# Decoder layer on one core: cross-attention queries and keys projected compactly and spread into 32-row strips through DRAM, queries one step ahead, blank rows written over three steps

## The reference

```
q = x1  @ q_w + q_b      # x1, ctx: [8, 256, 256]
k = ctx @ k_w + k_b      # 16 heads of 16 features
v = ctx @ v_w + v_b
a = softmax(q k^T / sqrt(16))          # per head, 256 x 256
x2 = layernorm(x1 + (a v) @ o_w + o_b)
# then: logits = x2 @ gate_w, best 2 of 8 experts, rows of x2 sorted by expert
```

## Time and profile before

| | |
|---|---|
| median of 3 runs | 996.15 us (994.75 to 998.77) |
| span of the profiled execution | 1000.6 us, 18366 instructions |
| PE busy in it | 883.4 us (88%) |
| DVE, ACT, POOL busy | 632.2, 431.9, 343.5 us |
| the slowest and only core's granted clock, mean | 0.946 |
| DMA | 123.54 MB, mean 123 GB/s |

### The profile page before, as it was taken

One profiled execution on the slowest core, in us unless ns is written; L12 is line 12 of the kernel. 1 busy time (PEld: TensorE's weight loads), 2 busy tenths in 40 slices (PEclk: granted clock), 3 DMA queues, 4 the chain that ended last, 5 costly groups with the idle time before them and its releaser, 6 DMA issues.

```text
span 1000.6 us, 18366 instructions
## 1 busy us (share of the span) xinstructions
PE 883.4 (88%) x6859; PEld 660.2 (66%) x6859; DVE 632.2 (63%) x1488; ACT 431.9 (43%) x781; POOL 343.5 (34%) x318
## 2 busy tenths in 40 slices
PE   7799788779889898889889998979997999999995
PEld 5576566657667675668656555555785777777774
DVE  5799797667898888752656778774553343333255
ACT  5688565335545544433134444445331322222221
POOL 9322201022555455620201223223631142222584
PEclk9899999868997977999989999999998999999998
DMA  5699679996454323212895112000402222221421
GB/s 167 193 273 282 192 174 242 294 225 144 100 112 74 81 49 74 62 49 90 325 388 188 51 56 85 23 23 25 155 10 89 60 64 64 60 62 55 148 65 63
DMA packets 144631, 123.54 MB, mean 123 GB/s; under 512 B 89952, under 2 KB 126752, under 8 KB 143264
## 3 DMA queue, kind: packets, MB, share of 16 engines
q1 hardware_dynamic: 141136, 112.99, 40.1%
q0 software_dynamic: 3408, 9.38, 2.5%
HBM read 74.05 MB, written 48.29 MB: 122 GB/s over the span
## 4 chain that ended last, share of the span: by engine, by line
PE 62%; DVE 16%; POOL 7%; ACT 6%; issue 4%; DMA 3%; SPq 1%; POOLq 0%; DVEq 0%; ACTq 0%
PE ps L2507 9%; PE ps L1913 6%; PE ps L2522 5%; DVE cross_room L1946 3%; PE ps L2371 3%; PE ps L1348 3%; PE ps L1853 3%; PE ps L666 3%; PE ps L2384 2%; POOL hank L345 2%; PE ps L1975 2%; PE ps L1614 2%; POOL kept L2654 2%; PE ps L423 2%; PE ps L1356 2%
## 5 line engine op out<-in xcount | busy, mean ns | idle before, releaser
L1991 ACT ACTIVATE cross_room<-ps 128x1024 f32<-128x1024 f32 x64 | 65.5, 1024 | 98.1 <-PE ps L1917 98.1
L1946 DVE TENSOR_REDUCE cross_room<-ps 128x4 f32<-128x1024 f32 x64 | 78.0, 1223 | 38.8 <-PE ps L1913 38.0
L2507 PE MATMUL ps<-wr,xbT 128*128 x312 | 100.6, 465 | 1.8 <-ACT xbT L2543 1.8
L1913 PE MATMUL ps<-kept,cross_room 32*128 32x256 f32 x512 | 73.3, 407 | 21.8 <-DVE cross_room L1946 18.8
L2596 POOL DMA_INDIRECT y_dram<-yb,dest_row x39 | 37.6, 963 | 136.2 <-DVE dest_row L2572 132.0
L1316 POOL TENSOR_TENSOR st<-st,exponent 128x20 f32<-128x20 f32 x16 | 56.6, 3535 | 69.1 <-DVE st L1291 67.8
L2507 PEld LDWEIGHTS ps<-wr,xbT 128*128 128x128 f32 x312 | 59.3, 191 | 30.1 <-issue 3.5
L1917 PE MATMUL ps<-cross_room,kept 32*128 32x256 f32 x512 | 74.5, 409 | 0.0
L1913 PEld LDWEIGHTS ps<-kept,cross_room 32*128 32x128 f32 x512 | 46.7, 188 | 39.6 <-issue 19.1
L550 DVE SCALAR_TENSOR_TENSOR room<-room 128x256 f32<-128x256 f32 x144 | 58.3, 477 | 11.6 <-ACT room L499 11.6
L2581 DVE TENSOR_TENSOR cross_room<-cross_room,ps 128x352 f32<-128x352 f32 x39 | 20.3, 521 | 60.3 <-PE ps L2507 58.9
(11 more groups left out here) (349 smaller groups left out, 2261.1 us busy)
## 6 DMA issues: line engine op xcount, KB each, us to landing
xs_dram<-params SPq DMA_DIRECT2D x17, 1040.0 KB, 17.8
room<-in_gW SPq DMA_DIRECT2D x8, 1280.0 KB, 8.0
tok_dram<-room SPq DMA_DIRECT2D x8, 768.0 KB, 6.3
fir_dram<-room SPq DMA_DIRECT2D x6, 1024.0 KB, 7.2
paths<-fir_dram SPq DMA_DIRECT2D x48, 128.0 KB, 3.8
xb<-xs_dram SPq DMA_DIRECT2D x39, 130.0 KB, 2.4
hank<-rt_dram SPq DMA_DIRECT2D x8, 512.0 KB, 7.6
yr<-y_dram SPq DMA_DIRECT2D x16, 256.0 KB, 3.3
```

The lines of the kernel that those rows point to most:

```text
L1913: m1 = nc.tensor.matmul(ps[:, c, t * T:(t + 1) * T], strips(qS[b % 3], g, c)[:, t * P:(t + 1) * P], kS(b, g)[c * CH:(c + 1) * CH], start=T ...
L1946: V.tensor_reduce(mx[:, :, g, XD + 2 * h * CH:XD + (2 * h + 1) * CH + 1:CH].rearrange("p t c -> p c t"), ps[:, pair(h), :].rearrange("p c ...
L1991: S.activation(pT[g % 2][:, pair(h)].rearrange("p c k t -> p (c k t)"), ps[:, pair(h), :].rearrange("p c n -> p (c n)"), ACT.Exp).then_inc ...
L2507: m = nc.tensor.matmul(ps[:, 2 * (j % 2) + half, 0:FF], xbT[j % 2][:, k, :], wr[:, bass.ds(e, 1), k, half, :].rearrange("p e n -> p (e n)" ...
```

## The change

Weights are no longer padded. One batch of queries or keys is 4 matmuls into `staged[b % 2]` (128 partitions x 2 x 256 tokens, feature-major, contiguous heads). SP writes these 256 KB to DRAM in two DMAs of 64 partitions (`sp_strips_out`), waits, and reads the padded form, 512 KB in one DMA, into the strips (`sp_strips_in`). The blank and one rows of the padded form are written to DRAM once, from a tile that POOL makes (`pool_pad`, `sp_pads`). In the delta and gate phase, keys 0 to 6 are written out and keys 0 to 4 fetched; batch 0's tokens are transposed and its queries projected there too. After the meeting SP issues the fetch of queries 0, the write of keys 7, the fetches of keys 5 to 7. In cross attention the queries of batch `b + 1` are made in the step that makes the maxes of batch `b` (`ahead`), which leaves 11 steps in place of 12; their one projection stands ahead of slot 3. SP's list of a step is: weights of an expert, tokens of a batch from 4 on, write of the queries, wait, fetch of the queries, and in the first three steps a third of the blank rows each (6, 6 and 5 DMAs of 1040 KB, and the one of 130 KB).

```diff
-    env.Ws = {"q_w": env.top("sq_w", [P, KT, XG, P]), "k_w": views(env.params, 3 * n_x, n_s, "p (k g n) -> p k g n", k=KT, g=XG)}
+    env.staged = [env.top(f"staged{i}", [P, KT, T]) for i in range(2)]
...
+def pool_pad(pg, env, made):
+    G.memset(env.pad, 0.0).then_inc(*pool.tick(made))
+    for c in range(NCH):
+        pool.in_turn()
+        G.affine_select(out=env.pad, in_=env.pad, compare_op=ALU.not_equal, fill=1.0, base=-(c * CH + XD), pattern=[[0, XG * T]],
+                        channel_multiplier=1).then_inc(*pool.tick(made))
+
+def sp_pads(pg, env, c, landed):
+    nc, zeros, rows = pg.nc, slice(c * CH, c * CH + XD), slice(c * CH + XD, (c + 1) * CH)
+    nc.sync.dma_start(env.k_pad[:, c, XD:].rearrange("b r g t -> r b (g t)"),
+                      env.pad[rows].unsqueeze(1).broadcast_to([CH - XD, B, XG * T])).then_inc(*landed.up(16))
+    nc.sync.dma_start(env.q_pad[:, c, XD:].rearrange("i r g t -> r i (g t)"),
+                      env.pad[zeros].unsqueeze(1).broadcast_to([CH - XD, 2, XG * T])).then_inc(*landed.up(16))
+
+def sp_strips_out(pg, pad, staged, landed):
+    for u in range(2):
+        pg.nc.sync.dma_start(pad.rearrange("c r (j u) t -> u c r j t", u=2)[u][:, 0:XD], staged[HS[u]]).then_inc(*landed.up(16))
+
+def sp_strips_in(pg, strips, pad, landed):
+    pg.nc.sync.dma_start(strips, pad.rearrange("c r g t -> (c r) g t")).then_inc(*landed.up(16))
...
+        def pe_heads(name, w, src):
+            for j in range(KT):
+                for k in range(KT):
+                    m = nc.tensor.matmul(kv_bank(name)[:, j * T:(j + 1) * T], w[:, k, j * P:(j + 1) * P], src[:, k, :], start=(k == 0),
+                                         stop=(k == 1))
...
         def act_keys(b):
+            act.wait_ge(s.k_made, b + 1)
+            act.wait_ge(kv.k_out[b % 2], 32 * (b // 2))
+            for j in range(KT):
+                m = S.activation(env.staged[b % 2][:, j, :], kv_bank(f"K{b}")[:, j * T:(j + 1) * T], ACT.Identity, bias=env.bk[:, j:j + 1])
...
-        sp_beside = {9: sp_context(0, 1), 10: sp_context(2, 3, 4), 11: sp_last()}
+        sp_beside = {9: rounds({0: ((C, 0), (C, 1))}),
+                     10: rounds({0: ((C, 2), (C, 3), (X, 0)), 1: ((out, 0),), 2: ((C, 4),),
+                                 3: ((out, 1), (C, 5), (out, 2), (back, 0), (back, 1))}),
+                     11: rounds({0: ((out, 3), (X, 1), (X, 2), (X, 3), (C, 6), (sp_query, 0), (back, 2)), 1: ((C, 7),),
+                                 2: ((out, 4), (back, 3), (out, 5), (back, 4)), 3: ((out, 6),)})}
...
         def sp_queries(b):
-            if b >= 4:
+            if 4 <= b < B:
                 copied(sp, "y", b - 4)
                 nc.sync.dma_start(xin[b % 4][:], batch(env.x1_dram, b)).then_inc(*x_in[b % 4].up(16))
-            yield
+            for _ in range(4):
+                yield
+            if b < B:
+                copied(sp, "q", b)
+                sp.wait_ge(kv.q_in[b % 2], 16 * (b // 2))
+                sp_strips_out(pg, env.q_pad[b % 2], env.staged[b % 2], kv.q_out[b % 2])
+                sp_query_in(b)
+            sp_blank(b - 1)
+            yield
+
+        def sp_query_in(b):
+            sp.wait_ge(kv.q_out[b % 2], 32 * (b // 2 + 1))
+            sp.wait_ge(s.p2_made, SLOTS * (b - 2))
+            sp_strips_in(pg, qS[b % 3], env.q_pad[b % 2], kv.q_in[b % 2])
...
         def pe_scores(b, slot):
             if b < B:
-                copied(pe, f"q{g // 2}", b)
+                pe.wait_ge(kv.q_in[b % 2], 16 * (b // 2 + 1))
+                pe.wait_ge(kv.k_in[b % 2], 16 * (b // 2 + 1))
...
-        def sp_blank():
+        def sp_blank(step):
+            if step > 2:
+                return
             sp.wait_ge(s.blank, 2)
-            for k in range(0, times, 2):
+            for k in range(12 * step, min(12 * step + 12, times), 2):
                 nc.sync.dma_start(places[:, k:k + 2], blank.unsqueeze(1).broadcast_to([P, 2, BLANKS, XW])).then_inc(*s.blank_out.up(16))
...
+        def sp_first():
+            sp_query_in(0)
+            sp_keys_out(pg, env, B - 1)
+            for b in range(5, B):
+                sp_keys_in(pg, env, b)
...
-        sp_before = {0: sp_blank} | {e + 2: lambda e=e: sp_weights(e) for e in range(NE)} | {B + 2: sp_last}
-        weave([sp_queries, idle, idle, idle, idle], B, sp_before)
-        weave([pe_queries, pe_maxes, pe_attend, pe_output, pe_place], B, {B + 2: lambda: free(pe)}, beside(firsts.pe(tokens)))
+        sp_before = {0: sp_first} | {e + 1: lambda e=e: sp_weights(e) for e in range(NE)} | {B + 1: sp_last}
+        weave([ahead(sp_queries), idle, idle, idle], B, sp_before)
+        weave([ahead(pe_queries, pe_maxes), pe_attend, pe_output, pe_place], B, {B + 1: lambda: free(pe)}, beside(firsts.pe(tokens)))
```

More of the change, by code:

```diff
@@ L811, in pool_cross_parameters @@
[L811 removed]
+CROSS_IN, PADS_IN = 16 * 9, 16 * 2 * NCH
+def pool_pad(pg, env, made):
     G, pool = pg.nc.gpsimd, pg.pool
[L814 to L820 removed]
@@ L1555, in pool_project_out @@
             yield
-        copied = env.kv.copied0 + env.kv.copied1
+        copied = s.copied0 + s.copied1
         turn = {}
-        for name in ["c0"] + [f"{part}{b + (part == 'c')}" for b in range(B) for part in ("c", "K", "k", "v")]:
-            turn[name] = len(turn)
+        for name in ["c0"] + [f"{part}{b + (part == 'c')}" for b in range(B) for part in ("c", "x", "K", "v", "q")]:
+            if name[0] in "cKv" or name in ("x1", "q3"):
+                turn[name] = len(turn)
+        x0T, q0 = views(flat(paths[2][:].rearrange("p n t d -> p n (t d)")), 0, n_x, "p (k t) -> p k t", 2, k=KT)
         def kv_bank(name):
@@ new lines, in pe_turn_first, with pe_first_query @@
+        def pe_turn_first(_):
+            pe.wait_ge(kv.x_in0[0], 16)
+            kv_free(pe, "x1")
+            for c in range(KT):
+                for t in range(TT):
+                    m = nc.tensor.transpose(kv_bank("x1")[:, (c * TT + t) * P:(c * TT + t + 1) * P],
+                                            env.xin[0][:, t, c * P:(c + 1) * P], ident[:])
+            m.then_inc(*s.x0_turned.up())
+        def pe_first_query(_):
+            kv_await(pe, "x1")
+            kv_free(pe, "q3")
+            pe_heads("q3", env.Wx["q_w"], x0T).then_inc(*s.q0_made.up())
@@ new lines, in act_turn_first, with dve_first_query @@
+        def act_turn_first(_):
+            act.wait_ge(s.x0_turned, 1)
+            act.wait_ge(s.gate_step, 16 * 5 + 12)
+            act.wait_ge(s.mix, 3 * 6)
+            S.copy(flat(x0T), kv_bank("x1")).then_inc(*kv_copied("x1").up())
+        def dve_first_query(_):
+            dve.wait_ge(s.q0_made, 1)
+            for j in range(KT):
+                m = V.tensor_scalar(q0[:, j, :], kv_bank("q3")[:, j * T:(j + 1) * T], env.bq[:, j:j + 1], XD ** -0.5, ALU.add, ALU.mult)
+            m.then_inc(*kv_copied("q3").up())
@@ L1606, in pe_keys_values @@
         def pe_keys_values(b):
-            pe.wait_ge(s.cross_made, CROSS_MADE)
             pe.wait_ge(s.cross_in, CROSS_IN)
             kv_await(pe, f"c{b}")
-            for half, name in enumerate((f"K{b}", f"k{b}")):
-                kv_free(pe, name)
-                for g in range(2):
-                    for k in range(KT):
-                        m = nc.tensor.matmul(kv_bank(name)[:, g * T:(g + 1) * T], env.Ws["k_w"][:, k, 2 * half + g, :], cT[b % 2][:, k, :],
-                                             start=(k == 0), stop=(k == 1))
-                m.then_inc(*kv.k_made.up())
+            kv_free(pe, f"K{b}")
@@ L1841, in pe_queries @@
         def pe_queries(b):
+            if b == B:
+                return
             yield
@@ L1846, in pe_queries @@
             yield
-            for half in range(2):
-                yield
-                copied(pe, "xT", b)
-                pe_shared(f"q{half}", b)
-                for g in range(2):
-                    for k in range(KT):
-                        m = nc.tensor.matmul(bank(f"q{half}", b)[:, g * T:(g + 1) * T], Ws["q_w"][:, k, 2 * half + g, :], xT[:, k, :],
-                                             start=(k == 0), stop=(k == 1))
-                m.then_inc(*s.q_made.up())
-                yield
+            yield
+            copied(pe, "xT", b)
+            pe_shared("q", b)
+            for j in range(KT):
+                for k in range(KT):
+                    m = nc.tensor.matmul(bank("q", b)[:, j * T:(j + 1) * T], Wx["q_w"][:, k, j * P:(j + 1) * P], xT[:, k, :],
+                                         start=(k == 0), stop=(k == 1))
+            m.then_inc(*s.q_made.up())
+            yield
         def act_queries(b):
+            if b == B:
+                return
             yield
-            act.wait_ge(s.x_turned, b + 1)
-            act.wait_ge(s.q_made, 2 * b)
+            act.wait_ge(s.x_turned, b)
+            act.wait_ge(s.q_made, b - 1)
             S.copy(flat(xT[:]), bank("xT", b)).then_inc(*out_of("xT", b).up())
@@ L1865, in dve_queries @@
         def dve_queries(b):
```

(14 more changed lines are left out.)

182 lines of the change are left out of this document (86 added, 96 removed).

## The result

The changed kernel takes 1018.33 us (median of 4 runs, 1015.95 to 1023.07) against 995.45 us for the kernel before beside it: ratio 1.0239, 95% interval 1.0192 to 1.0286. I forecast 997.0 us, range 985 to 1003, with 0.19 for slower. The time lies 15 us above the range. The profiled execution of the changed kernel has a span of 1014.1 us; its time is 1015.95.

The account below looks back on a forecast made before the run. What binds depends on the stage: PE in the gate tail; PE and waits for maxima in full steps; full DMAs from 478. Gate tail -8.9 and cross attention +9.8 gave +0.9 on span 1001.5, less 4.45: 997.0 us, range 985 to 1003.

Parts of the forecast that it names:

- the landing of the compact writes: Key and query writes to DRAM: land 2.2 us after issue, so ACT's key copies, with about 8 us, do not wait.
- Half-partition writes of 1 KB rows: Writes beside the blanks, priced by no profile row: would act like landings under load 2 us dearer each.
- the price of the clock: Cross attention: PE's clock falls after idling; 2 us added for the long wait and 1 for the start.
- Gate tail: Before the meeting: halved key matmuls, less batch 0's added queries, gain 2.2 + 6.9 = 9.1 us, taken as 8.9.
- The gate tail gives half: Rival, before the meeting: ACT or PE waits for SP's list, gain only 4.4 us, time 1001.5; chance 0.09.
- Queries 1: Start of step 1: copied at m + 10.2, fetched by m + 16.8, due at m + 17 (m: meeting's end).
- The chain to the tokens: Cross attention, steps 0 to 3: query writes, fetches and blanks in turn; batch 4's tokens land at m + 81.5.
- Tokens behind the blanks: Step 3: batch 4's tokens wait for the bytes of blanks and weights issued ahead; PE waits 13 us.
- Slot 4 to 5: Full cross attention steps: second query half gone, 2.80 us for 3.44, gain 0.64 us a step.
- First scores under 4 us after the meeting: Start of cross attention: fetch of queries 0 lands after 3.7 us, scores at m + 3.8, gain 1.3 us.
- The costless parts: POOL's four selects (bounds 4 to 34.4 us, low end taken) and 2.6 MB of pads cost nothing; uncovered pads 7 us.
- The rival of dear landings: Cross attention: q2, q3 and tokens each land 2 us later under load, 6 us more, time 1003; chance 0.13.

Follow-up runs that it names:

- the mended one: Changed kernel with batch 4's tokens ahead of the last blanks, 16-entry compact write, keys 6 behind x1 of batch 7, pads earlier: 988.39 us, ratio 0.9922; again 0.9943.
- the keys put back: The mended one with the matmuls of each batch's keys done twice: 1000.54 us, ratio 1.0040.
- the wide write: Changed kernel with compact queries and keys written with slowest DRAM-side dimension 16 in place of 4, and 2 KB rows: 1010.34 us, ratio 1.0120.
- the other order of keys 6: Changed kernel with the write of keys 6 moved behind the write of x1 of batch 7: 1013.49 us, ratio 1.0157.
- the experiment above: The mended one with eight more matmuls, results unread, at the start of cross attention: 990.46 us, ratio 0.9958.
- the version with more of them: The mended one with the eight unread matmuls, plus one ahead of slots 1 to 7 of step 0 and three ahead of step 1: 993.99 us, ratio 0.9956.

## Why the prediction was wrong, point by point

**The step that failed** is the landing of the compact writes. The prediction says of ACT's key copies that they "wait for the write of the keys two batches before: that has about 8 us, and takes 2.2 us", and of queries 1 "two issues and 2.2 to land", at m + 13; both times 2.2 us was the row of x1's write, taken over by its 256 KB alone. The write has another shape, its slowest dimension on the DRAM side has 4 entries, and it lands after 4.5 to 4.7 us with the queue empty and 8.29 us after its issue with contexts and fetches around it. I had named "Half-partition writes of 1 KB rows" as a price in no row, looked at rows and partitions, and not at the order of the dimensions. Both signs that I had set for being wrong came: a wait for the query fetch at the start of step 1, and key copies of ACT waiting for DMA. Three terms rest on it, the third for the smaller part; the second step that failed is the price of the clock.

- *Gate tail*, forecast -8.9, measured -2.2. The working was right for a kernel in which the write does not hold the tail: the mended one gains 8.1 and 8.5 us, and the keys put back take 8.3 away again. In the kernel as it was changed the key copies of ACT waited 4.6 us for the slow writes, and x1 of batch 7 landed behind them, after 6.7 us where the wide write leaves it 2.4. No run has the wide write without either the wait for the pads or the other order of keys 6, so the two are not told apart further. My rival "The gate tail gives half" had the right place, and asked for too little (a gain of 4.4; it was 2.2).
- *Queries 1*, forecast "fetched by m + 16.8" and "just covered", measured m + 23.2 (490.31 - 467.1), a wait of 5.03 us. These 6.4 us are 2.9 for the copy (through at m + 13.1, 480.24 - 467.1, in place of m + 10.2, in a step at a clock of 0.51), 0.6 for the issues, 2.3 for the write (4.54 for 2.2) and 0.6 for the fetch. So the write is 2.3 of the 6.4; the copy is late by the clock and by what stands ahead of it. With the wide write and all mended, 1.91 us of the wait are left.
- *The chain to the tokens*, forecast to end at m + 81.5, measured m + 93.6 (560.67). Step 0 takes 19.6 us in place of 13.2 and step 1 28.5 in place of 26.2, so queries 3 are copied 8.5 us later; the landing of their write then is 8.1 us, behind blanks and weights, in DRAM at m + 71.7 in place of m + 61. The last 1.4 us lie in blanks and tokens. The narrow write is the smaller part of this: with the write wide and nothing done to the tokens they come at m + 89.9 (562.27 - 472.33), so 3.6 of the 12.1 us go and 8.4 stay. That version's steps 0 and 1 are still longer than forecast, at a mean clock of 0.78 and 0.76.

**Tokens behind the blanks**: right. Forecast 13 us, measured 15.65, gone when the load is moved up, and 3.25 for two blanks. The load took 12.7 us from issue, not 19, as SP was itself slow in issuing what stands ahead (8.7 us, 539.20 to 547.93, for eight DMAs); from the issue of the fetch of queries 3 it is 21.8 us, and I had 20.5 (m + 61 to m + 81.5). The load waits for the bytes issued ahead of it, as the prediction had from the earlier trace rows. One slip runs through these sums: they take a KB as 1000 bytes, and the profile's is 1024 (256 KB are 256 x 256 floats). A blank is 2.74 us of the full DMAs and six are 16.4, not 16.0; and the bytes ahead of the weights of 512.26 end at 527.6, not 526.5, so that they landed 1.6 us behind the last byte, less than the lone 1.9: the 0.8 us of load that the prediction read there are not there.

**Slot 4 to 5** at 2.80: right. 572.61 to 575.42 is 2.81 us, the last 1.12 of them waiting for DVE, as in the earlier trace rows. In the mended kernel two full steps with no wait for a DMA take 25.9 and 27.9 us, for 26.6 and 28.6 before: 0.6 and 0.7, forecast 0.64.

**First scores under 4 us after the meeting**: right, 3.6 (forecast 3.8). The fetch landed after 3.5 us; the 3.7 of the prediction is more than its rows give (3.3 to 3.5). The gain was eaten at once: from 468 to 478 the clock was at 0.51.

**The clock** had 3 us in the forecast, 2 for the long wait and 1 for the start, and that was too little. Cross attention has some 48 us of low clock in five stretches after, 10 before. How much of the 21.1 us it makes cannot be read off by itself, since PE mostly waits in them; with the wide write alone, cross attention is at 240.7, still 7.4 of the 11.3 us above the forecast, with 41 us of low clock; in the mended kernel it takes 223.7 us (228.3 in the other profile) where forecast gains of 5.6 would have given 218, with 27 us of low clock (31), of which the stretch behind the meeting, 10 us at 0.50 (7), is one that the kernel before lacks. What brings the clock down stays open: each long fall came behind idle time of PE, and the experiment above could not remove the idle time ahead of the first.

**The costless parts.** POOL's four selects took 4.85 us, near the low end, and its next work did not move (209.93 us, before 209.90). The pads cost nothing that shows in the kernel as changed. They were far from costless three steps later, 7 to 8 us of PE waiting for a context: their cover was their place, not the share of the DMAs.

**The numbers.** Misses: 6.7 us in the tail, 11.3 in cross attention, 2.4 in the experts, 20.4 together, against 21.3 between forecast and result. The likeliest case had 0.60. The rival of dear landings ended at 1003, because it added 2 us three times, to landings under load; the dear landing was in the write itself, which all 16 writes of keys and queries share, and most in those without load (4.66 for 1.73 us, against 8.1 for 7.5 behind blanks).

## What to carry to other kernels

A DMA's price is not that of another with as many bytes: before taking over a row, put both access patterns side by side, the slowest dimension of each side first (4 entries against 64 partitions: 70 GB/s and a share of 0.24). A slow small write harms not only through its own wait but through what stands behind it on the same queue: here an unchanged write of x1 went from 2.2 to 6.7 us, at the meeting of all engines, and back to 2.4 when the writes ahead of it were wide. And a load that will be needed soon goes ahead of bulk writes whose landing nobody awaits: the price of leaving it behind them is their bytes, 2.5 us for each blank here.

## What the runs showed that I had not expected

- The same 256 KB landed after 4.66 us with a slowest dimension of 4 and 1 KB rows, 4.14 with 4 and 2 KB rows, 1.73 with 16 and 2 KB rows.
- The granted clock fell to 0.51 while PE was busy 7.00 of 7.00 us; it had been at 1.00 in the 5.9 us before, of which PE was busy the first 3.72 and then idle for 2.26.
- With PE busy throughout step 0, step 1 ran at a mean clock of 0.87 in place of 0.81.
- With the eight added matmuls, and nothing else changed, the first scores began 6.0 us after the fetch of queries 0 was issued (469.09 - 463.08), and 5.9 in the version with more of them, against 3.95 without. It is the landing of the fetch that is later. I can't say why; it is enough to cancel what a better clock could have given.
- The profiled span before A, in which no version differs but for POOL's and some DMA work, varied by 9.5 us between executions (414.2 to 423.65), and by 6.7 between two of one and the same kernel (415.54 and 422.24), more than the effect of several edits here: parts are to be compared, not spans.
